# Counting edges with one-hot products: products divided where new columns begin, two plain batches first, lane tables byte by byte on GpSimd

## The reference

```
HW = x @ W;  s = HW @ a[:512, 0];  t = HW @ a[512:, 0]
e = leaky_relu(s[src] + t[dst], 0.2)
m = segment_max(e, src);  ex = exp(e - m[src])
att = ex / segment_sum(ex, src)[src]
agg = segment_sum(att[:, None] * x[dst], src)
out = silu(agg) @ base_w.T + einsum('nip,oip->no', splines(agg), spline_w)
return layernorm(x + out)
```

## Time and profile before

| What | us |
|---|---|
| median of 3 runs (393.06 to 393.66) | 393.36 |
| the profiled execution's own time | 394.73 |
| its span | 392.9 |
| TensorE busy in it | 374.4 (95%) |
| VectorE busy | 338.2 (86%) |
| ScalarE busy | 249.1 (63%) |
| GpSimd busy | 40.0 (10%) |

### The profile page before, as it was taken

How to read it: one execution, slowest core, us unless ns; L and a number is a source line. 1 busy time by engine, 2 the same in 40 slices (tenths; PEclk the granted TensorE clock), 3 DMA queues, 4 the chain that set the end, 5 groups by cost and what they waited for, 6 DMA issues and landing times.

```text
span 392.9 us, 5137 instructions
## 1 busy us (share of the span) xinstructions
PE 374.4 (95%) x1914; PEld 301.2 (77%) x1914; DVE 338.2 (86%) x450; ACT 249.1 (63%) x243; POOL 40.0 (10%) x96
## 2 busy tenths in 40 slices
PE   4699789999999999999999999999999999999994
PEld 1466547888888888778888888888888888888883
DVE  7977699997677598999899999889999899989345
ACT  6466644454445979865786766687758696866222
POOL 7200221000000001001010101001010101001000
PEclk9999999999999999999999999999999999999999
DMA  7910970600000036549646455623423454633302
GB/s 228 392 39 32 235 131 10 206 0 2 0 3 0 0 108 214 160 122 306 188 112 180 138 162 159 197 72 77 138 62 98 135 159 135 219 97 79 84 27 101
DMA packets 23914, 47.21 MB, mean 120 GB/s; under 512 B 1932, under 2 KB 2348, under 8 KB 23890
## 3 DMA queue, kind: packets, MB, share of 16 engines
q0 software_dynamic: 12416, 24.00, 24.0%
q1 hardware_dynamic: 11474, 22.89, 17.8%
HBM read 44.31 MB, written 2.57 MB: 119 GB/s over the span
## 4 chain that ended last, share of the span: by engine, by line
PE 91%; DVE 4%; issue 3%; POOL 1%; DMA 1%; DVEq 0%; ACT 0%; POOLq 0%
PE PS L1425 63%; PE PS L1368 18%; PE PS L1308 5%; PE PS L1350 3%; PE PS L1378 1%; DVE oh L566 1%; PE PS L1265 1%; PE PS L1285 1%; DMA ei<-in_edges 1%; PE PS L1242 0%; DVE scrap L763 0%; DVE still L553 0%; POOL lp L454 0%; DVE Z L710 0%; POOL gk L452 0%
## 5 line engine op out<-in xcount | busy, mean ns | idle before, releaser
L1425 PE MATMUL PS<-wh,s 128*128 128x512 f32 x720 | 223.0, 390 | 0.1
L1425 PEld LDWEIGHTS PS<-wh,s 128*128 128x128 f32 x720 | 135.1, 188 | 29.6 <-issue 1.6
L1425 PE MATMUL PS<-wl,s 128*128 128x512 f32 x360 | 140.1, 389 | 0.0
L1425 PEld LDWEIGHTS PS<-wl,s 128*128 128x128 f32 x360 | 67.6, 188 | 13.8
L1163 ACT ACTIVATE s<-v 128x1280 fp32r<-128x1280 f32 (+1 forms) x32 | 40.1, 1252 | 42.2 <-DVE v L948 23.8
L1146 ACT ACTIVATE v<-xt,bias 128x1280 f32<-128x1280 f32 (+1 forms) x32 | 42.9, 1340 | 18.3 <-DVE s L958 17.2
L942 DVE SCALAR_TENSOR_TENSOR v<-v,v 128x1280 f32<-128x1280 f32 (+1 forms) x32 | 46.4, 1451 | 6.3 <-ACT v L1149 6.3
L948 DVE SCALAR_TENSOR_TENSOR v<-v,v 128x1280 f32<-128x1280 f32 (+1 forms) x32 | 46.8, 1461 | 3.7 <-DVE v L944 0.5
L958 DVE SCALAR_TENSOR_TENSOR s<-v,s 128x1280 fp32r<-128x1280 f32 (+1 forms) x32 | 46.5, 1454 | 3.1 <-ACT s L1163 3.1
L500 POOL DMA_DIRECT2D wh<-in_splT x32 | 22.9, 715 | 256.8 <-PE PS L1425 183.8
L944 DVE SCALAR_TENSOR_TENSOR v<-v,v 128x1280 f32<-128x1280 f32 (+1 forms) x32 | 46.5, 1453 | 0.0
(11 more groups left out here) (166 smaller groups left out, 333.7 us busy)
## 6 DMA issues: line engine op xcount, KB each, us to landing
wh<-in_splT POOLq DMA_DIRECT2D x32, 512.0 KB, 4.2
wring<-in_splT SPq DMA_DIRECT2D x21, 512.0 KB, 4.0
xt<-in_xT SPq DMA_DIRECT2D x1, 2500.0 KB, 12.5
xh<-in_x POOLq DMA_DIRECT2D x1, 2304.0 KB, 10.8
out<-xr SPq DMA_DIRECT2D x9, 256.0 KB
wh<-in_baseT POOLq DMA_DIRECT2D x4, 512.0 KB, 5.4
wring<-in_baseT SPq DMA_DIRECT2D x3, 512.0 KB, 4.9
xr<-in_x SPq DMA_DIRECT2D x1, 1280.0 KB
```

The lines of the kernel that those rows point to most:

```text
L1425: m = e.matmul(PS[:, w % 8, :], sx[:, ic, tl * 128:tl * 128 + 128], wx[:, ic, :], start=first and n == 0, stop=last and n == 2)
```

## The change

- **Products.** `cleared` and `WARM_AT` are gone. All products into a window's first tile are issued with `start=True` (overwrite). In later tiles `parts_of` divides each stretch where columns begin that no earlier tile has reached, so that a product either adds everywhere or writes fresh columns everywhere. The number of products goes from 259 to 424, with nearly the same sum of columns (47820 and 47916).
- **Groups.** Batches 0 and 1 are single and plain (`PLAIN`), batch 6 takes the place of batch 5 on ScalarE, single batches at the end are 19 and 20 (before 18, 19 and 20). There are still 13 groups. The still matrix stays a plain bf16 comparison for groups 0 to 5 (batches 0 to 8), and comes from lanes only from group 6 on (`ROWS_IN_LANES`).
- **Tables.** `pat8` and `row8` are written by GpSimd, each with eight `tensor_scalar` operations on 176 int32 values (equal to k, times 0x38, the byte of 1.0 in fp8) into every eighth byte. `gk` is copied by ScalarE instead of GpSimd.
- **Zero products first.** 14 zero products (`keep_warm(14)`) stand ahead of the first group instead of the six clearings.
- **Places.** `ends_along`, `st_rows`, `s_column`, ScalarE's copies, `marks` and the `left_...` steps move by one group or batch; the load of `r_size` moves from behind group 10 to behind group 9; seven instead of nine negations stand in the loop of batches; `greatest_of(0)` in the loop over leftovers also waits for `s_scol`.

The diff, cut to its core:

```diff
-BY_SCALAR = 5
-SINGLE = (0, BY_SCALAR, NB - 3, NB - 2, NB - 1)
+BY_SCALAR = 6
+PLAIN = (0, 1)
+SINGLE = PLAIN + (BY_SCALAR, NB - 2, NB - 1)
...
+IN_LANES = [b not in PLAIN + (BY_SCALAR,) for b, _ in GROUPS]
+ROWS_IN_LANES = [b > BY_SCALAR + 2 for b, _ in GROUPS]
...
+def reached(t, w):
+
+    return max((hi for u in range(t) for v, lo, hi in stretches(u) if v == w), default=CW * w)
+
+
+def parts_of(t):
+
+    parts = []
+    for w, lo, hi in stretches(t):
+        old = min(max(reached(t, w), lo), hi) if t > FIRST_TILE[w] else lo
+        parts += [(w, a, b) for a, b in ((lo, old), (old, hi)) if a < b]
+    return parts
...
-        LOADS_AT = NB - 3
+        LOADS_AT = NG - 4
 
-        NEGATIVE_AT = {10 + k: k for k in range(NT - 1)}
+        NEGATIVE_AT = {11 + k: k for k in range(NT - 3)}
...
-        MARKS_AT = {7: (8,), 8: (10, 12), 9: (14,), 10: (16,), 11: (18,)}
-        WARM_AT = range(11, NB - 2)
+        MARKS_AT = {8: (8,), 9: (10, 12), 10: (14,), 11: (16,), 12: (18,)}
...
+            def lane_bytes(table, key):
+
+                for k in range(LANES):
+                    m = e.tensor_scalar(table[:, :, k], key, float(k), float(ONE_IN_8), ALU.is_equal, ALU.mult)
+                m.then_inc(s_table, 1)
+
             e.wait_ge(s_ln, 2)
-            e.tensor_copy(lp[:, :, :], ln[:, :].unsqueeze(2).broadcast_to([128, NCP, 2])).then_inc(s_gk, 1)
-            e.tensor_copy(rk[:, :, :], ri[:, :].unsqueeze(2).broadcast_to([128, NCP, 2])).then_inc(s_gk, 1)
-            e.tensor_copy(rp[:, :, :], rl[:, :].unsqueeze(2).broadcast_to([128, NCP, 2])).then_inc(s_gk, 1)
+            lane_bytes(pat8, ln[:, :])
...
+            e.wait_ge(s_rk, 2)
+            lane_bytes(row8, rl[:, :])
...
-                if g == 1:
-                    e.wait_ge(s_pat, 2)
+                if g == len(PLAIN):
+                    e.wait_ge(s_table, 1)
...
-            one_hot_still()
-            moving()
-            for g in range(1, NG):
-                if g == 1:
-                    e.wait_ge(s_gk, 3)
+            for g in range(NG):
                 if IN_LANES[g]:
                     hits(g)
...
-                if g == 6:
+                if g == 7:
                     most_of_tiles()
                 if g == 8:
                     most_of_halves()
...
-                touches(g)
-                if g == 1:
-                    e.wait_ge(s_gk, 4)
-                    lane_table(row8, rp)
-                    lane_table(pat8, lp)
-                    e.wait_ge(s_pat, 1)
-                rows_in_lanes(g)
+                for w in MARKS_AT.get(g, ()):
+                    e.wait_ge(s_cnt, taken(w + 1))
+                    marks(w, w + 2).then_inc(s_filled, 1)
+                if ROWS_IN_LANES[g]:
+                    touches(g)
+                    rows_in_lanes(g)
+                else:
+                    one_hot_still(g)
...
-            for w in range(6):
-                cleared(w)
+            keep_warm(14)
...
-                    for w, lo, hi in stretches(t):
-                        if w >= 6 and t == FIRST_TILE[w]:
+                    for w, lo, hi in parts_of(t):
+                        if w >= 6 and lo == FIRST_OF[w] and t == FIRST_TILE[w]:
                             e.wait_ge(s_hole if w - 6 < BY_EVACUATION else s_cnt, taken(w - 6))
-                            cleared(w)
-                        m = e.matmul(PS[:, w % 6, lo - CW * w:hi - CW * w], held[:, k, :],
-                                     moved[:, k, lo - o:hi - o], start=False, stop=(t == LAST_TILE[w]))
+                        m = e.matmul(PS[:, w % 6, lo - CW * w:hi - CW * w], held[:, k, :], moved[:, k, lo - o:hi - o],
+                                     start=(t == FIRST_TILE[w]), stop=(t == LAST_TILE[w]))
                     m.then_inc(s_ct, 1)
-                if b in WARM_AT:
-                    e.matmul(PS[:, w % 6, 0:CW], nought[:, 0:128], nought[:, 0:CW], start=False, stop=False)
...
-                if g == 4:
+                if g == 5:
                     ends_along()
-                if g in (4, 5):
-                    st_rows(2 * g - 8)
-                    st_rows(2 * g - 7)
+                if g in (5, 6):
+                    st_rows(2 * g - 10)
+                    st_rows(2 * g - 9)
```

More of the change, by code:

```diff
@@ L79 @@
 LAST_TILE = [max(t for t in range(NV) if w in [p[0] for p in stretches(t)]) for w in range(ND)]
+FIRST_OF = [next(p[1] for p in stretches(FIRST_TILE[w]) if p[0] == w) for w in range(ND)]
+def reached(t, w):
[6 more added lines that the diff above has]
+    return parts
 NP = 8
@@ L175, in build @@
         xt0 = at("xt0", 19, [128, 4, RP])
-        oh = [at(f"oh{k}", 23 + k, [128, TB, MV], BF16) for k in range(RB)]
+        oh = [at(f"oh{k}", 23 + k, [128, TB, MV], BF16) for k in range(len(PLAIN))]
+        oh_by = at("oh_by", 18, [128, TB, MV], BF16)
         oh8 = [at(f"oh8{k}", 23 + k, [128, 2 * TB, MV], F8) for k in range(RB)]
@@ L236, in build @@
         s_setup = sem("s_setup")
[L237 to L240 removed]
+        s_table = sem("s_table")
+        s_row_key = sem("s_row_key")
+        (s_reach, s_bits, s_col, s_mk, s_bound, s_left, s_tab, s_mi, s_ln, s_rk, s_hit, s_row, s_filled, s_mv, s_head, s_ovk, s_ovm, s_ovs, s_ova, s_ovz, s_marked, s_early, s_near, s_touch, s_first, s_next, s_begun, s_late, s_tmax, s_small, s_z, s_p, s_den, s_rden, s_plo,
          s_a3, s_b3, s_spl, s_slo, s_wlo, s_res, s_bns, s_bna, s_rstd, s_nb, s_fin) = (
             sem(f"v_{n}") for n in (
[L243 removed]
+                "reach", "bits", "col", "mk", "bound", "left", "tab", "mi", "ln", "rk", "hit", "row", "filled", "mv", "head", "ovk", "ovm", "ovs", "ova", "ovz", "marked", "early", "near", "touch", "first", "next", "begun", "late", "tmax", "small", "z", "p", "den", "rden", "plo",
                 "a3", "b3", "spl", "slo", "wlo", "res", "bns", "bna", "rstd", "nb", "fin"))
[L246 removed]
+        (s_lk, s_gk, s_by_mk, s_off, s_by, s_sq, s_neg, s_war, s_wa, s_srow, s_trow, s_scol, s_cnt, s_hole, s_gentle, s_ex, s_phi, s_ya, s_ev, s_abs, s_q2, s_a2,
          s_silu, s_shi, s_root, s_fina) = (sem(f"a_{n}") for n in (
[L248 removed]
+             "lk", "gk", "by_mk", "off", "by", "sq", "neg", "war", "wa", "srow", "trow", "scol", "cnt", "hole", "gentle", "ex", "phi", "ya", "ev", "abs", "q2", "a2",
              "silu", "shi", "root", "fina"))
@@ L747, in _ @@
                     lanes(g)
-                if g == 1:
+                elif g < len(PLAIN):
+                    moving(g)
+                if g == 2:
                     least_and_most()
-                for w in MARKS_AT.get(g, ()):
-                    e.wait_ge(s_cnt, taken(w + 1))
-                    marks(w, w + 2).then_inc(s_filled, 1)
                 if g == 8:
                     left_limits()
-                if GROUPS[g][0] == LOADS_AT:
+                if g == LOADS_AT:
                     e.wait_ge(s_tab, TABLE)
@@ L1045, in moving_by_scalar @@
                     e.wait_ge(s_off, part + 1)
-                    e.activation(oh[GROUP_OF[b] % RB][:, part * k:part * k + k, 0:2 * h], off[:, :, :], ACT.Relu, bias=1.0,
+                    e.activation(oh_by[:, part * k:part * k + k, 0:2 * h], off[:, :, :], ACT.Relu, bias=1.0,
                                  scale=-1.0).then_inc(s_by, 1)
```

95 lines of the change are left out of this document (49 added, 46 removed).

## The result

| What | us |
|---|---|
| changed kernel, median of 4 runs (400.86 to 401.23) | 401.01 |
| kernel before, median of 4 runs (393.06 to 394.29) | 393.51 |
| ratio | 1.019, 95% interval 1.017 to 1.021 |
| the profiled execution's own time, its span | 401.08, 399.3 |

The prediction said 388.4 and 0.88 for faster. It was wrong by 12.6 us and in sign, and the measured time lies 9.7 us above its range (386.9 to 391.3).

The account below looks back on a forecast made before the run. VectorE's arrival at the loop over leftovers was taken to bound what the change can move: 49.75 to 44.3 us, -5.4, counted as -5.0 after a 0.45 correction, so the median goes from 393.36 to 388.4 us; range 386.9 to 391.3.

Parts of the forecast that it names:

- Mark A: TensorE begins the first paired group; forecast at about 11.9 us against 13.63 before, if GpSimd's first table is ready at 10.7.
- upper bound, 1.2: Highest price kept for one GpSimd table operation, in us, if reading, comparing and writing single bytes cost double; 0.6 was taken.
- the 1.14 at which all gain is gone: Price in us of one GpSimd table operation at which, both tables being late, the forecast gain vanishes.
- Rival 1: GpSimd's byte operations are slow, both tables late; 394.5 us at 1.2 each; chance 0.21, of it 0.07 slower.
- Rival 2: TensorE's clock falls in a gap of some 2.8 us before group 10; 389.3 to 390.2 us; chance 0.10.
- Rival 3: Products are bound by their number, not columns; 390.8 us, or 394.1 by the skill's figure; chance 0.08.
- Rival 4: VectorE loses nothing to GpSimd, so 0.9 us of slack in moving and hit terms goes; 387.5 us; no separate chance.
- mark B: VectorE passes the second transpose (L661); forecast at 28.4 us against 35.40 before.
- From B to C: VectorE from the second transpose to the loop over leftovers; forecast 15.9 us against 14.35 before, ending at 44.3.
- 2.9 idle as before: VectorE's idle time in us ahead of group 10, since the load of the sizes takes 4.2 and 1.3 runs beside it.
- `trow` and `gentle` stayed hidden: Under what costs nothing: these loads, 8.0 and 9.6 us after `strow`, forecast ready by 38.8 for a reader at 44.3.
- the signs named beforehand: Traces to tell right from wrong, such as `tensor_scalar` at 0.5 to 0.7 us, or TensorE waiting over 2 us for tables.

## Why the prediction was wrong

**The step that failed** is in Mark A, "I take 0.6, beside VectorE, and keep 0.2 and 1.2". The operation takes 1.04 us alone and 1.32 and 1.74 on the mean of each table. Both 0.2 and 0.6 are half of what a copy of 352 elements takes from start to start, 0.43 while VectorE waits and 1.20 beside it, "if time follows them". But a copy is no measure for arithmetic: 176 numbers in two steps cost 0.80 alone in any type, over three times what an element costs a copy, and bytes eight apart 1.04, five times the 0.2. The factor of contention was read rightly: copies took 2.6 times as long beside VectorE (1.25 against 0.48), and 1.04 times it is 2.7, near what operations beside a steady VectorE took (2.81). So the term that was mis-sized is the bare price of the operation. The prediction's own upper bound, 1.2, lay beyond the 1.14 at which all gain is gone, yet no gain or a loss by this rival got a chance of 0.09 in all.

**Rival 1 was the right mechanism**, with a chance of 0.07 for slower. It put 394.5 at 1.2 us an operation and 1.6 for each further 0.1; at the mean of 1.53 that is 399.8, and 401.0 was measured. That it comes so near is in part luck: it lacks 2.1 us of clock and holds 2.7 us too much for the load of the sizes (below), and these cancel. **Rival 2** expected the fall of the clock ahead of group 10, where it didn't come (gap of 1.41, granted clock 1.00, the 42 products took 2.44); it came in the gaps that rival 1 opens, for 2.1 us. Two rivals were priced as if each came alone, and one causes the other.

**Rival 3 fell.** 43 products of two batches took 2.56 us and 40 with fewer columns 2.20; a product costs some 8 to 10 ns beyond its columns, not 3.5, so two batches take 2.5 instead of 2.27. The Trainium skill, "TensorE: Matmul & The Clock Gate", section "Back-to-back issue gap", by which 43 products would be an estimated 3.5 us, doesn't hold for these; the 2.56 decides. **Rival 4** held in part: VectorE's walk from its first still matrix to its first wait took 5.12 us beside GpSimd, not the 5.44 of the forecast, and further on it lost about 0.4 us in 8, so contention falls almost wholly on GpSimd. The Trainium skill, "GPSIMD Engine Reference", section "Engine selection", whose advice spoke against the change, was right: the operation takes 0.22 us on VectorE and 1.04 on GpSimd. The best case in the Trainium skill, same page, section "Elementwise — side-by-side cycle accounting", 1.8 cycles an element, an estimated 0.26 us an operation, is a quarter of the measured 1.04.

**The rest of the working stood.** With the tables on VectorE the forecast of mark A would be 11.9 + 1.76 = 13.66, measured 13.65; mark B 28.4 + 1.76 = 30.16, measured 30.25. That these agree to 0.1 is partly luck: VectorE began 0.40 later (5.62) and walked 0.52 faster (4.92 instead of 5.44) up to the table; TensorE began group 5 0.3 earlier behind mark A than forecast, and took 0.4 longer from there. From B to C it was 15.9, and 13.2 in every kernel with the new order: the "2.9 idle as before" for the load of the sizes became 0.18, since the load took 1.42 us there instead of 4.22. In the changed kernel:

```profile
L311 DVEq TENSOR_LOAD <-r_size x1: 1423/1423/1423, 48.2 to 48.2; - x1
```

So that term was mis-sized by 2.7 in the other direction: with an idle time of 2.9 there, the miss would have been some 15 us instead of 12.6. `trow` and `gentle` stayed hidden, as forecast.

Of the signs named beforehand, two spoke: TensorE waiting over 2 us for lanes of group 2 (6.64) and rows of group 6 (5.94), and GpSimd's `tensor_scalar` far from 0.5 to 0.7.

## What to carry to other kernels
Before work is moved to an idle engine, measure that very operation there; a copy on the same engine says nothing of arithmetic, and a quiet stage nothing of a busy one. Write down how long one piece may take before it is felt (here 0.72 us) and, if neither end of your bounds is safe, let the chance follow the bounds. A wait of several us in front of TensorE can cost twice, since its clock may fall in the gap: behind the second gap this cost 2.4 us more, behind the first nothing. Price such rivals together.

## What the hardware showed that was not expected
- The same operation on 176 numbers: 0.22 us on VectorE, 1.04 on GpSimd alone, and up to 4.50 beside a busy VectorE, whether the DMAs are busy or not. VectorE loses about 0.4 us in 8.
- What VectorE does matters. Beside its fp32 layer norm the dense forms took 0.80 to 0.83 us, against 0.80 alone; beside its last spline operation, fp32 too, and a DMA, a spread one took 1.83 instead of 1.05; beside the one-hot comparisons and products of the counting stage up to 4.50. Which of VectorE's operations hold GpSimd up wasn't tried one by one.
- The load of five numbers into VectorE's registers took 4.22 us in the order of before, 3.12 in it with divided products, and 1.41 to 1.42 in all kernels with the new order, with whole products too. What in the order sets it wasn't tried apart.
